# Node places loaded at the end of the first layer's sums, and the first batch's scores ahead of the second layer's start

## What is computed

```python
# layer 0: sums of transformed neighbours
neighbours = segment_sum((x @ w1)[src], dst)
x = layernorm(x + relu(x @ w0 + neighbours))
# layer 1: attention with 8 heads of 32, weights by edge type
h_all  = einsum('nf,rof->rno', x, W)
scores = einsum(h_all[type, src], attn_src) + einsum(h_all[type, dst], attn_dst)
scores = where(scores > 0, scores, 0.2 * scores)
amax   = maximum(segment_max(scores, dst), 0)
w      = exp(scores - amax[dst]);  w = w / segment_sum(w, dst)[dst]
out    = segment_sum(h_all[type, src] * w, dst)
x = layernorm(x + out)
```

## Time and profile before

| | us |
|---|---|
| median of 3 runs | 2754.34 |
| lowest and highest run | 2751.61, 2757.78 |
| span of the profiled execution | 3067.8 |

### The profile page before, as it was taken

The page is one execution under the profiler, slowest core; times in us unless marked ns, Lnnn a source line. Parts: engine busy times, 40 slices in busy tenths (PEclk is TensorE's granted clock), DMA queues, the critical chain, the costliest instruction groups (busy, mean ns, idle before and its releaser), DMA issues.

```text
span 3067.8 us, 38107 instructions
## 1 busy us (share of the span) xinstructions
PE 2357.8 (77%) x9936; PEld 1676.6 (55%) x9936; DVE 1943.7 (63%) x4273; ACT 1618.7 (53%) x3465; POOL 1840.7 (60%) x1875
## 2 busy tenths in 40 slices
PE   8786688899999989999981667766776667766675
PEld 3455566666666666666651545444554555554541
DVE  9893656554555555545530767767777777677787
ACT  4573455655555555555540555555655555455543
POOL 1004766677777767776617566666666666666625
PEclk9897899999999999999985777878878788687788
DMA  5103446644444444444533444444444444444424
GB/s 155 49 13 113 123 122 161 211 146 143 146 136 142 141 146 142 144 141 144 135 138 105 107 128 120 122 123 117 133 121 120 122 120 124 118 130 122 118 69 142
DMA packets 177777, 387.53 MB, mean 126 GB/s; under 512 B 42669, under 2 KB 106867, under 8 KB 171042
## 3 DMA queue, kind: packets, MB, share of 16 engines
q0 software_dynamic: 83888, 233.09, 28.3%
q1 hardware_dynamic: 86626, 99.05, 10.6%
q10 hardware_dynamic: 7056, 52.99, 4.5%
HBM read 302.96 MB, written 82.03 MB: 125 GB/s over the span
## 4 chain that ended last, share of the span: by engine, by line
PE 51%; DVE 18%; issue 15%; another core or an unknown queue 8%; ACT 3%; DVEq 2%; POOL 1%; DMA 1%; SPq 0%; ACTq 0%; POOLq 0%
PE ps L1695 22%; PE ps L1811 11%; PE ps L1745 10%; DVE nodes L895 6%; PE ps L1794 3%; DVE nodes L777 2%; DVE region L884 2%; PE ps L1664 1%; ACT region L1461 1%; PE ps L1652 1%; DVE edge_z L1029 1%; DVEq L895 1%; ACT region L1465 1%; DVE region L868 1%
## 5 line engine op out<-in xcount | busy, mean ns | idle before, releaser
L1303 POOL DMA_INDIRECT region<-y_d,edge_z x856 | 875.0, 1022 | 571.4 <-issue 231.4
L1348 POOL DMA_INDIRECT region<-ha_d,idx_t x880 | 891.7, 1013 | 495.3 <-issue 242.7
L777 DVE TENSOR_TENSOR nodes<-ps,nodes 128x512 f32 x856 | 591.8, 691 | 616.0 <-PE ps L1695 333.2
L1695 PE MATMUL ps<-region 128*128 128x256 f32 x3424 | 830.1, 394 | 134.7 <-issue 72.8
L1811 PE MATMUL ps<-region 128*128 128x264 f32 x1760 | 645.0, 502 | 279.5 <-DVE nodes L895 114.1
L1695 PEld LDWEIGHTS ps<-region 128*128 128x128 f32 x3424 | 654.2, 196 | 343.4 <-issue 207.3
L1811 PEld LDWEIGHTS ps<-region 128*128 128x128 f32 x1760 | 370.2, 237 | 467.1 <-issue 177.8
L895 DVE TENSOR_TENSOR nodes<-ps,nodes 128x264 f32 x880 | 374.0, 425 | 304.6 <-remote 207.1
L1461 ACT ACTIVATE region<-iota_n,edge_z 128x256 f32<-128x256 f32 x856 | 364.7, 500 | 62.7 <-PE ps L1695 40.3
L1745 PE MATMUL ps<-region,edge_z 128*128 128x512 f32 x784 | 366.8, 598 | 12.5 <-ACT edge_z L1491 7.5
L1503 ACT COPY region<-ps 128x512 f32<-128x512 f32 x196 | 114.2, 586 | 403.2 <-PE ps L1745 169.5
(11 more groups left out here) (265 smaller groups left out, 1826.8 us busy)
## 6 DMA issues: line engine op xcount, KB each, us to landing
ha_d<-region ACTq DMA_DIRECT2D x49, 1056.0 KB
region<-near_d SPq DMA_DIRECT2D x55, 512.0 KB
region<-ha_d,idx_t POOLq DMA_INDIRECT x880
region<-y_d,edge_z POOLq DMA_INDIRECT x856
edge_z<-level_d SPq DMA_DIRECT2D x55, 136.0 KB
kl_d<-region SPq DMA_DIRECT2D x8, 903.0 KB
edge_z<-kl_d SPq DMA_DIRECT2D x55, 129.0 KB
y_d<-edge_z SPq DMA_DIRECT2D x25, 256.0 KB, 3.2
```

Of the source, the lines that this page charges most:

```text
L777: v.tensor_tensor(into, ps[:, u, :], into, ALU.add).then_inc(added0, 1)
L1303: g.indirect_dma_start(rows0[c % RING][:, u, :], None, y_d, bass.IndirectOffsetOnAxis(ap=y_idx[:, k:k + 1], axis=0), bounds_check=node_bou ...
L1348: g.indirect_dma_start(rows[s][:, k, :], None, ha_rows, bass.IndirectOffsetOnAxis(ap=idx_t[:, B * b + k:B * b + k + 1], axis=0), bounds_ch ...
L1695: mm = t.matmul(ps[:, u, h * D:(h + 1) * D], lhsT=sel0[c % SEL][:, u, h * P:(h + 1) * P], rhs=rows0[c % RING][:, u, :], start=True, stop=True)
```

## The change

SP loads the places of the first two batches as soon as the first layer's column sums have ended (`segs0` at COLS) and only then waits for `begun`. ScalarE makes the first batch's four quarters of one-hots in rounds 235 to 238 of the first layer's loop, one behind that round's copies. TensorE computes the first batch's destination scores after it has seen the last table copied and before it waits for `begun` and raises `segs` by 64. Rounds -2 and -1 of the second layer leave the first batch's part out. So that the early tiles don't stand on what the end of the first layer still uses, `near_b` and `st` move to the end of the second layer's part of `region`, behind the first layer's table tiles.

```diff
@@ region
+        early_at = o + 2 * R * AW
...
-        near_b = [view(region, o + B * P // 2 * h, B * P // 2).bitcast(BF16) for h in range(2)]; o += B * P
-        st = [view(region, o + 4 * P * q, 4, P) for q in range(4)]; o += 16 * P
         prod = view(region, o, 8, H, R); o += 8 * RH
         bsel = [view(region, o + P * h, B, H) for h in range(2)]; o += 2 * P
         tmask = [view(region, o + B * R * h, B, R) for h in range(2)]; o += 2 * B * R
         z_c = [view(region, o + P * h, B, H) for h in range(2)]; o += 2 * P
+        assert o >= early_at
+        near_b = [view(region, o + B * P // 2 * h, B * P // 2).bitcast(BF16) for h in range(2)]; o += B * P
+        st = [view(region, o + 4 * P * q, 4, P) for q in range(4)]; o += 16 * P
@@ SP
-            sp.wait_ge(begun, 1)
...
+            sp.wait_ge(segs0, COLS)
             load_places(0, 0)
             load_places(1, 1)
+            sp.wait_ge(begun, 1)
             in_pairs(sp, 0, NB - 2, load_ahead)
@@ ScalarE, the first layer's loop (node_one_hots is now defined ahead of it)
             for c in range(NG + LATE + 1):
...
+                if NG + LATE - 4 <= c < NG + LATE:
+                    node_one_hots(0, c - (NG + LATE - 4))
@@ ScalarE, the second layer's rounds
-                p, c, summing, ahead = is_batch(i + 1), is_batch(i), is_batch(i - 1), is_batch(i + 2)
+                p, c, summing = is_batch(i + 1), is_batch(i), is_batch(i - 1)
+                ahead = is_batch(i + 2) and i + 2 > 0
...
-                if p:
+                if p and i + 1 > 0:
                     node_one_hots(i + 1, 3)
@@ TensorE
             t.wait_ge(unit_copied, NU)
-            t.wait_ge(begun, 1)
-            t.sem_inc(segs, 64)
...
+            for half in range(2):
+                halves_at[0, half] = tiles_of(0, half)
+                destination_scores(0, 2 * half)
+                destination_scores(0, 2 * half + 1)
+            t.wait_ge(begun, 1)
+            t.sem_inc(segs, 64)
...
-                p, c, a, o, ahead = is_batch(i + 1), is_batch(i), is_batch(i - 1), is_batch(i - 2), is_batch(i + 2)
+                c, a, o = is_batch(i), is_batch(i - 1), is_batch(i - 2)
+                p, ahead = is_batch(i + 1) and i + 1 > 0, is_batch(i + 2) and i + 2 > 0
```

More of the change, by code:

```diff
@@ L1515, in copy_unit, with node_one_hots @@
                     a.copy(b_sb[:, ds(jobs[t] * (2 * RH) + h * RH, RH)], ps[:, bank, RH:2 * RH]).then_inc(unit_copied, 1)
+            def node_one_hots(b, q):
+                if q == 0:
+                    a.wait_ge(near_in[b % 2], 16 * (b // 2 + 1))
+                if b:
+                    a.wait_ge(b_made, 4 * b + q - 3)
+                to = st[q].rearrange("p u e -> p (u e)")
+                a.activation(to, near_b[b % 2][:, 4 * P * q:4 * P * q + 4 * P], ACT.Abs, bias=part[:, 0:1],
+                             scale=-1.0).then_inc(st_near, 1)
+                a.wait_ge(st_near, 4 * b + q + 1)
+                a.activation(to, to, ACT.Relu, bias=ones[:, 0:1], scale=-1.0).then_inc(st_made, 1)
             unit = 0
@@ L1785, in tiles_of @@
                 return [t.snap(r, min_val=0, max_val=NT - 1) for r in regs]
+            halves_at = {}
             def destination_scores(b, q):
@@ L1812, in sum_edges @@
                              start=True, stop=True).then_inc(segs, 1)
-            halves_at = {}
             def batch(i):
                 h = i % 2
-                p, c, a, o, ahead = is_batch(i + 1), is_batch(i), is_batch(i - 1), is_batch(i - 2), is_batch(i + 2)
+                c, a, o = is_batch(i), is_batch(i - 1), is_batch(i - 2)
+                p, ahead = is_batch(i + 1) and i + 1 > 0, is_batch(i + 2) and i + 2 > 0
                 if p:
```

## The result

The changed kernel takes 2763.07 us (median of 20 runs), the kernel before 2758.64 (20 runs, among them the three shown). The ratio is 1.0016, 95% interval 1.0009 to 1.0023: slower by 4.4 us. That is more than nothing; whether it is less than 0.2% the interval leaves open. The forecast was 2757.2, 2.9 us over a base of 2754.34, with a range up to 2763.0. Kind and sign of the delay were as forecast; the base was 4.3 us too low, and one term of the delay 0.8 too small.

What follows compares the result with a forecast made beforehand. The prediction took the first batch's 16 gathers to bound the seam: earlier places, one-hots and scores gain nothing, while the release comes 2.9 us later. So 2754.34 + 2.9 = 2757.2 us, 8-in-10 range 2738 to 2763.

Steps and rivals of the forecast that it cites:

- the base: Whole kernel: median of the timed runs before the change, 2754.34 us, to which the predicted delay was added.
- The first batch waits for its 16 gathers: Seam between the layers: GpSimd's gathers cover the places' load, one-hots and scores, so bringing these forward gains nothing.
- GpSimd and everything behind its gathers starts later by that: Second layer: the 2.9 us later start of the gathers carries through all the rest, +0.1%.
- the forecast of 1555.5: End of the column sums: SP issues both 512 KB place loads then, landing by about 1561, at no cost.
- This is on the path: Last ha_d store: one pair of one-hots ahead of it takes 1.39 us, making `begun` 1.4 us late for GpSimd.
- I estimate 4.2 us for all of it: TensorE's sequencer before the release: register loads (0.78 and 0.59 us), register instructions and gaps, putting line 1778 at 1599.0.
- The bounds of 1.4 and 6.7: Gathers' delay: 1.4 us if the sequencer's part hides beside the store's landing, 6.7 if the release waits for the matmuls.
- the late tellings: TensorE results there but signalled late, with the lull's issue pieces 323 us; taken as a profiling cost absent from timed runs.
- The profiled span itself may shrink by 10 to 60 us: Changed kernel's profile: waits belonging to profiling would be cut, without contradicting the forecast.
- The stalls are real: Rival, chance 0.22: score calls crawl while gathers pour in, in timed runs too; early scores gain 17.3 us, 2737 us.
- The release waits for the matmuls: Rival, chance 0.13: line 1778 runs only after the 32 score passes, so gathers start 6.7 us late, 2761.0 us.
- Nothing happens: Rival, chance 0.07: second pair and calls fit beside the last store's landing and gathers aren't the pace; 2754.3 us.

Runs made afterwards that it cites:

- the eleven later executions: Profiled executions after the one the prediction read: the kernel before again, the change, and nine repeats or edited kernels; ratios to the kernel before from 0.9996 to 1.0119.
- the pairs behind the store: Against the change: the four pairs of one-hots moved out of the loop, behind the last store and last copy; ratio to the kernel before 1.0012.
- the release first: Against the change: TensorE waits for begun and raises segs ahead of its register loads and four score calls; ratio to the kernel before 1.0002.
- the kernel before's second profile: The kernel before, unedited, profiled once more; ratio 0.9996, span 2756.4 us in an execution of 2758.24.
- 20 calls: Also "16 calls more": against the change, 16 further score calls by TensorE ahead of the release; ratio to the kernel before 1.0119.
- the change three times: The change, its unedited repeat, and the change with 16 extra register loads that weren't in the program that ran; ratios to the kernel before 1.0016, 1.0017, 1.0010.
- the loads hoisted: Against the change: TensorE's two register loads of the first batch put ahead of its wait for the copied tables; ratio to the kernel before 1.0008.

## Why the prediction was right and wrong

**Right: what bounds the seam.** "The first batch waits for its 16 gathers" holds: in the eleven later executions line 938 or 940 is let go by the gathers, 8.7 to 19.6 us after VectorE was ready. In the profile that the prediction read, the row itself names VectorE's own line 874, 0.80 us before, because the scores were so late there that they ended beside the gathers; the prediction passed over that. But line 938 starts 22.89 us behind the first gather there too, where the others have 22.85 to 22.94. Early places won 4.4 us at the scores and nothing at line 938. "GpSimd and everything behind its gathers starts later by that" is shown from 5.70 to 37.52 us of start: rest less first gather lies between 1262.7 and 1265.4 in all eleven.

**Right: the places and the store.** SP's first load is at 1445.45, 35.0 us before the last full copy; the forecast of 1555.5 was 35.2 before it. That they cost nothing is as forecast, too. The store was to be 1.39 late and is 1.35. "This is on the path" doesn't hold in the change, where it hides beside TensorE's stream, as the kernel with the pairs behind the store shows; it comes out only with the release first (1.36). The 2.9 went by TensorE's sequencer and not by this.

**Wrong: a term of the sum.** "I estimate 4.2 us for all of it, from the sum of 2.25 and about as much again for issue" is the step of the delay that failed. TensorE's sequencer came free at 4.2 us behind the copy (forecast 4.15), but the release took 5.0 more: the first register load ran 1.43 us, where I had put in 0.78. The gathers are therefore 3.71 us late, not 2.9. The bounds of 1.4 and 6.7 held it. That the start agrees so well is luck: 1595.1 less 0.63 is 1594.5 and not 1594.8 (3.8 behind the copy), and twice 2.25 would be 4.5; the two slips cancel in the 1599.0.

**Wrong: the base.** "2754.34 + 2.9" rests on three runs; 20 runs have 2758.64, and the three weren't spread enough to show it. This term is the larger part of the miss: of 5.9 us, 4.3 are the base, 0.8 the register load and what goes with it, and 0.7 lie within the interval of the measured delay (2.5 to 6.3 us). On that base the same sum gives 2761.5, and 3.71 gives 2762.35, beside 2763.07 measured. The range's upper end, worked out from the same base, fell short by 0.07 us for this reason. That this kernel's runs "can't tell less than about 0.2%" came from the same three runs; 20 of each told 0.16% from nothing.

**Wrong: the cause of the late tellings.** I took them "for a cost of being profiled". Eleven further profiled executions have spans 1.8 us under their own times, which leaves no place for 323 us of stalls; so it wasn't profiling in general. The use that I made of it, not to count them, was right. "The profiled span itself may shrink by 10 to 60 us" was off for the same reason: it shrank by 314.

**The rivals.** *The stalls are real* falls with the kernel before's second profile: the third and fourth call do not crawl while gathers pour in; the two lines 868 stand 3.4 us apart there, and not 12.0. The Trainium skill's "Perfetto Trace Analysis", section "Tensor Engine Instruction", says that a matmul's end is estimated. Here the estimated end of the 32nd pass and the start of its reader, line 868, agree to 0.2 us in that second profile (1504.46 and 1504.67), so late real ends aren't seen. *The release waits for the matmuls* is not what happened: the release at 1489.7 stands ahead of the 32nd pass, about 1493.6 by 1486.60 + 32 x 0.218:

```profile
1486.60 12.20 PE L1799 MATMUL ps<-edge_z,region 128*128 x56 [4.73 <-ACT region L1528]
```

With 20 calls it is what happens. *Nothing happens* is excluded by both measurements of the change.

## What to carry to other kernels

Ask of each wait on a chain which other input of the same consumer ends last; here 8.7 us or more of gathers lay over everything that was brought forward. The start of the engine that paces this stage was worth its time one to one, so work that makes the release of such an engine later is paid for, even where it is free on its own engine. And a profile whose span is far over the timed runs should be read beside a second one of the same kernel, by distances from an event that both have.

## What was not expected

The first register load behind the last copy takes 1.43 us in four executions (the change three times, and with 16 calls more) and 1.96 to 1.97 in the two with the pairs behind the store, but 0.77 with the release first or the loads hoisted, and 0.59 in the median of 110. In the slow ones the last 1056 KB store was in flight, in the fast ones not; no run isolates that, and it stays open.

In these profiles most of the scatter of the time is made before the first layer's column sums end: the last full copy starts over a stretch of 11 us in the eleven later executions, always 42.1 us behind the last addition of a column sum, while the rest of executions with the same first gather lies within 2.7.
